# Expert results added straight into the output of a graph and mixture-of-experts layer

## The reference, cut to what matters

```python
edge_index = jnp.stack([src, dst])
xn = _layernorm(x, axis=-1)
x = x + _L0_gnn_ref(xn, edge_index, ...) + _L0_mix_ref(xn[None], ...)[0]
x = x + _L0_ffn_ref(_layernorm(x, axis=-1)[None], ...)[0]

# _L0_ffn_ref: S tokens, E = 8 experts, K = 2 chosen, D = 256, H = 1024
gate_scores = jnp.einsum('bsd,ed->bse', x, Wg) + bg
topk_scores, topk_idx = jax.lax.top_k(gate_scores, K)
topk_probs = jax.nn.softmax(topk_scores, axis=-1)
for e in range(E):
    h = jax.nn.relu(jnp.einsum('bsd,hd->bsh', x, W1[e]) + b1[e])
    y = jnp.einsum('bsh,dh->bsd', h, W2[e]) + b2[e]
    out = out + combine[..., e:e + 1] * y
```

## Time and profile before

| | us |
|---|---|
| median of 3 executions | 1453.89 |
| lowest and highest | 1453.29, 1457.96 |
| profiled execution, its own time | 1454.93 |
| its span, first to last instruction | 1452.8 |
| mean granted clock of PE | 0.907 |

### The profile page before, as it was taken

The page is one execution under the profiler, slowest core; times in us unless marked ns, Lnnn a source line. Parts: engine busy times, 40 slices in busy tenths (PEclk is TensorE's granted clock), DMA queues, the critical chain, the costliest instruction groups (busy, mean ns, idle before and its releaser), DMA issues.

```text
span 1452.8 us, 25219 instructions
## 1 busy us (share of the span) xinstructions
PE 1210.4 (83%) x7992; PEld 869.7 (60%) x7993; DVE 848.5 (58%) x1771; ACT 601.5 (41%) x1947; POOL 735.3 (51%) x626
## 2 busy tenths in 40 slices
PE   3789956758777877799999999365899999999994
PEld 2545533425444544455554556265799999999994
DVE  8598859788888887554545455697323222332221
ACT  1300011443444345487777777251333333333331
POOL 2070000788888888777777777550233333333331
PEclk9999966878899888999999999756999999999998
DMA  5635374422222223343343344583122222222223
GB/s 180 207 130 187 139 281 139 141 78 77 77 77 74 80 77 87 98 117 109 113 116 114 103 115 113 222 343 142 30 38 37 36 36 36 36 36 36 36 36 103
DMA packets 67569, 153.67 MB, mean 106 GB/s; under 512 B 12961, under 2 KB 41558, under 8 KB 66262
## 3 DMA queue, kind: packets, MB, share of 16 engines
q0 software_dynamic: 32640, 75.27, 21.0%
q1 hardware_dynamic: 33478, 74.93, 14.6%
q10 hardware_dynamic: 1360, 2.33, 0.5%
HBM read 131.76 MB, written 23.92 MB: 107 GB/s over the span
## 4 chain that ended last, share of the span: by engine, by line
PE 61%; DVE 21%; POOL 7%; issue 5%; DMA 4%; ACT 1%; DVEq 1%; SPq 0%; POOLq 0%; ACTq 0%
PE ps L1543 14%; PE ps L1553 13%; PE ps L1250 13%; POOL arena L847 6%; DVE arena L1809 6%; PE ps L1191 4%; PE ps L1446 3%; PE ps L1458 2%; PE ps L1279 2%; PE ps L1200 1%; PE ps L1158 1%; DMA h_d<-arena 1%; DVE arena L1769 1%; DVE arena L1777 1%; PE ps L1404 1%
## 5 line engine op out<-in xcount | busy, mean ns | idle before, releaser
L847 POOL DMA_INDIRECT arena<-h_d,tables x440 | 516.0, 1173 | 134.0 <-issue 131.3
L1250 PE MATMUL ps<-arena 128*128 128x264 f32 x880 | 251.3, 441 | 89.6 <-DVE acc L1818 61.6
L1250 PEld LDWEIGHTS ps<-arena 128*128 128x128 f32 x880 | 184.6, 218 | 149.0 <-issue 97.2
L964 ACT ACTIVATE arena<-arena 128x64 f32<-128x64 f32 x880 | 222.0, 338 | 37.1 <-DMA arena<-h_d,tables 37.1
L889 POOL DMA_INDIRECT sum_d<-acc,tables x56 | 89.7, 1601 | 253.4 <-DVE acc L2197 245.8
L1543 PE MATMUL ps<-acc 128*128 128x128 f32 x1792 | 210.2, 276 | 0.0
L1543 PEld LDWEIGHTS ps<-acc 128*128 128x128 f32 x1792 | 205.6, 193 | 0.1
L1553 PE MATMUL ps<-arena,acc 128*128 x896 | 202.5, 379 | 0.0
L1553 PEld LDWEIGHTS ps<-arena,acc 128*128 128x128 f32 x896 | 166.0, 190 | 20.3
L1120 ACT ACTIVATE acc<-ps,b_s 128x128 f32<-128x128 f32 x448 | 128.1, 369 | 119.0 <-PE ps L1543 119.0
L2185 DVE COPY acc<-arena 128x1024 f32 x112 | 78.2, 699 | 121.7 <-PE ps L1543 120.8
(11 more groups left out here) (366 smaller groups left out, 1532.7 us busy)
## 6 DMA issues: line engine op xcount, KB each, us to landing
arena<-dl_d SPq DMA_DIRECT2D x22, 640.0 KB, 7.2
arena<-lo_d SPq DMA_DIRECT2D x16, 784.0 KB, 4.6
arena<-h_d,tables POOLq DMA_INDIRECT x440
arena<-in_w SPq DMA_DIRECT2D x4, 1664.0 KB, 12.3
arena<-in_w SPq DMA_DIRECT2D x4, 1632.0 KB, 25.2
arena<-hi_d SPq DMA_DIRECT2D x16, 343.0 KB, 5.1
h_d<-arena SPq DMA_DIRECT2D x25, 128.0 KB, 2.0
sum_d<-res SPq DMA_DIRECT2D x5, 640.0 KB, 8.6
```

Source lines behind the costliest of these rows:

```text
L847: pool.indirect_dma_start(gb[u][:, k, 0:D], None, h_d, bass.IndirectOffsetOnAxis(tsrc[:, j:j + 1], 0)).then_inc(s_gg[u], 16)
L964: ins = A_.activation(v, v, ACT.Copy, scale=wm[:, m + k, h:h + 1])
L1250: last = MM(ps[:, 6 + s, 0:ACOL], oh[b % OB][:, m, :], gb[u][:, m, :], start=(k == 0), stop=(k == TE - 1))
```

## The change

The scratch tensor `sum_d` and its zero tile are gone. SP stores the residual rows into `out`: four chunks as before, and the fifth as two DMAs, four whole tiles and the 53 real rows of the last tile. The scatter goes to `out`, and it is given a bound: an index above N - 1 = 3124 is dropped by the DMA and is no error. The copy at the end goes. The waits for `s_res` now count the six stores, where they counted five; those for `s_zero` count one DMA, where they counted two.

```diff
-        sum_d = dram("sum_d", [NP + P, D])
...
             sp.dma_start(xn_d[NP:NP + P, :], zrow).then_inc(s_zero, 16)
-            sp.dma_start(sum_d[NP:NP + P, :], zrow).then_inc(s_zero, 16)
...
             for c in range(LC):
                 sp.wait_ge(s_att2, c + 1)
-                sp.dma_start(sum_d[c * LW * P:(c + 1) * LW * P, :].rearrange("(t p) c -> p t c", p=P),
-                             res[:, c * LW:(c + 1) * LW, :]).then_inc(s_res, 16)
+                a, b = c * LW, min((c + 1) * LW, NT - 1)
+                sp.dma_start(ot[:, a:b, :], res[:, a:b, :]).then_inc(s_res, 16)
+                if c == LC - 1:
+                    sp.dma_start(out[(NT - 1) * P:N, :], res[0:TAIL, NT - 1, :]).then_inc(s_res, 16)
                 if c:
                     store_normalized(c - 1)
...
-            sp.wait_ge(s_fy, 16 * NJ)
-            sp.dma_start(out.rearrange("n c -> (n c)").rearrange("(p w) -> p w", p=P),
-                         sum_d[0:N, :].rearrange("n c -> (n c)").rearrange("(p w) -> p w", p=P)).then_inc(s_res, 16)
             sp.wait_ge(s_res, 16 * (LC + 1))
...
-            pool.wait_ge(s_zero, 32)
+            pool.wait_ge(s_zero, 16)
...
-                pool.indirect_dma_start(sum_d, bass.IndirectOffsetOnAxis(pidx[:, j:j + 1], 0),
-                                        ys[j % 2], None, compute_op=ALU.add).then_inc(s_fy, 16)
+                pool.indirect_dma_start(out, bass.IndirectOffsetOnAxis(pidx[:, j:j + 1], 0),
+                                        ys[j % 2], None, bounds_check=N - 1, oob_is_err=False,
+                                        compute_op=ALU.add).then_inc(s_fy, 16)
             for j in range(JB - 1):
                 load_tokens(j)
-            pool.wait_ge(s_res, 16 * LC)
+            pool.wait_ge(s_res, 16 * (LC + 1))
...
-                dve.wait_ge(s_zero, 32)
+                dve.wait_ge(s_zero, 16)
...
             dve.wait_ge(s_xst, 16 * LC)
-            dve.wait_ge(s_res, 16 * LC)
+            dve.wait_ge(s_res, 16 * (LC + 1))
```

## The result

The changed kernel took 1448.51 us (median of 8 executions, 1445.38 to 1451.59), the kernel before 1453.59 us in the same set (8 executions). The ratio is 0.9963, 95% interval 0.9947 to 0.9979. In a second set of runs the same kernel gave 0.9952, 0.9936 to 0.9969. So it is faster, by 5 to 7 us (3 to 9 us by the intervals), where 12.5 us had been forecast: the time lies 4 us above the upper end of the range.

What follows compares the result with a forecast made beforehand. PE bounds the kernel to 1431 us, then the last two scatters, the copy and the program end. Copy 11.93 plus scatters 0.6 gives 12.5 us off 1453.89: 1441.4 us, own range 1440.2 to 1442.4, 8-in-10 range 1438.9 to 1444.6.

Steps and rivals of the forecast that it cites:

- The step that failed: Program end: without the copy, the last scatter lands at 1440.45 us and 0.42 us of end follow; gain 11.93 us.
- The prediction's own sign of being wrong: Program end: the forecast is wrong if the end lies over 1 us behind the last landing.
- The rival that named it: Program exit: it waits for something that the copy hid, nothing is gained, 1453.9 us; chance 1%.
- The two bare scatters: Last two scatters, on the path: bound costs at most +2.6 us, dropped rows give -2.1 us; taken as -0.6 us.
- The rule of the Trainium skill on a DMA issued by GpSimd: Last two scatters: about 2.0 us plus bytes at 436 GB/s; empty tile worth 0.3 us, both tiles 0.5 us.
- The cover in the loop: Expert loop: 54 of 56 scatters cost nothing; their landing may grow by 3.2 us before the next scatter waits.
- The tail store: Fifth residual store's extra issue on SP, about 975.5 us: free; as a rival, late, giving 1447.9 us, chance 4%.
- The other side: Loop, wait L887: bounded add into `out` becomes the loop's bound; about 1482 us at twice today's landing; chance 3%.

## Why the prediction was wrong, point by point

- **The step that failed** is "If the 0.42 us of program end stay, the span ends at 1440.45 + 0.42 = 1440.87". The copy's 11.9 us were read right, and that nothing busy stood beside it as well. But the 0.42 us were those of SP, the last engine to finish. Whose end would be last next, and how long it is, was not looked up. POOL's is 6.6 us, so the edit is worth 12.3 - 6.6 = 5.7 us and not 11.93. The kernel without the copy, the one with a short copy and the one without the DRAIN show it from three sides. The prediction's own sign of being wrong, an end over 1 us behind the last landing, is what came. With the gain at the scatters the sum would have been 5.7 + 0.7 = 6.4 us; measured by the medians were 5.1 and 6.9.
- **The rival that named it** had 1%: "the exit of the program waits for something that the copy hid". It was put as all or nothing. What was hidden is half as long as the copy, so half of the gain stayed. The range did not reach it.
- **The two bare scatters** were right in sum, within 0.2 us, and in the sign of each part; the forecast had given bounds for the parts and no sizes. From the end of DVE's L2197 for tile 54 to the last landing it was 8.4 us before and 7.7 us after; -0.6 had been forecast. The parts: +0.1 us of lag at the first and +0.5 us at the second (taken from 0.60 us of POOL's work in the forecast, but POOL's work did not grow; it is the start that is later), -1.0 us for the empty tile, of which 1.22 had been the bound, and -0.1 to -0.5 us over the bounded kernels for the one with 36 tokens, against up to 0.88, which took the saving to be in proportion to the rows.
- **The rule of the Trainium skill on a DMA issued by GpSimd** ("DMA: Bandwidth & Descriptors", "Anatomy of one DMA"), about 2.0 us and the bytes on top, agrees with the trace in that most of the cost stays when no row is moved, though that was 2.7 us. Its 0.3 us for 128 KB does not fit: the empty tile landed 1.0 us sooner than a full one, near the 1.22 us for which the DMA engines had been busy. These are accumulating writes of 1 KB rows, which the formula does not single out. Of the two, the busy time of the DMA engines was the nearer for an empty tile.
- **The cover in the loop** held. The scatter's landing had a median of 3.8 us as before, POOL waited for no landing but the one ahead of the last scatter, and the loop took 397.6 us (396.6 before), with two others of the changed form at 397.3 and 398.4.
- **The tail store** cost SP 0.36 us at 973.6, and DVE passed L2160 (now L2158) without idle time. It landed at 979.2, 5.5 us after its issue. The trace has the updates of the count `s_res`: the four-tile store beside it made sixteen, from 975.96 to 976.15 us, and the tail store two, one 0.5 us after its issue and one at 979.18. That agrees with one engine for all 53 rows, as the prediction had it, and the landing is far inside the 19.5 us that it had allowed.
- **The other side**, a loop bound by the landing of the scatters, did not occur.

## What to carry to other kernels

When the last thing of a program goes away, the new end is that of the engine that finishes next, with its own way out: list, for every engine, when it passes its last wait and what it still does after it, although none of it counts as busy. Here GpSimd, after 560 indirect DMAs, had a DRAIN of 6.27 us to pay at its end. It could be paid in small parts earlier, where the engine was idle, or in part beside the last landing when another engine did the waiting. A bound that drops unused rows also shortens the last, mostly empty transfer; it cost half a microsecond where the issue hung on a landing and 0.1 us where it hung on DVE (0.84 us from the end of DVE's L2195 to the scatter, 0.75 us before).

## What the runs showed of the hardware that was not expected

- GpSimd's DRAIN took 0.70, 2.17 and 4.62 us with 8, 26 and 56 indirect DMAs since the last DRAIN, a straight line of 0.082 us each (or of the time that they took), and 5.97 and 6.27 us with 109 and 560. That length counts from the end of POOL's own last issue. With over 450 behind it and gathers in flight, an early DRAIN ended 6.4 to 7.5 us after POOL's last issue.
- A DRAIN that has less than that to do still ends 0.28 to 0.36 us behind the last landing (14 DRAINs in one kernel), so its end does not come before that landing.
- In the loop an early DRAIN with its full length, about 6.4 us behind a gather, made the whole loop 3.5 us longer, of which PE waited 2.6 us for the next gather; DRAINs with 8 DMAs behind them in the same place, 2.1 to 2.7 us behind the gather, made it no longer.
- An indirect DMA with a bound starts 0.75 us behind the landing that it waits for, one without after 0.27 us, and POOL is busy 1.55 us for either, also when all 128 rows are dropped.
- Kernels that are the same up to their end differ by 1.7 us in the first turns of the expert loop. PE's first 32 products there took 4.61 us in the profile of before, at a mean granted clock of 0.80, and 6.28 and 5.51 us, at 0.58 and 0.66, in the kernels without the copy and with the short copy. The changed kernel's took 6.23 us at 0.58.
